# Gate sums of a cross-attention kernel: one accumulator over eight tiles, or two accumulators at output partitions 0 and 64

## What is computed

```python
q = _layernorm(x); k = v = ctx
xc = jnp.concatenate([q, k, v], axis=-1)
ig = (xc @ Wi + bi).transpose(0, 2, 1)[..., None]
fg = (xc @ Wf + bf).transpose(0, 2, 1)[..., None]
log_f = jax.nn.log_sigmoid(fg)
log_f_cum = cumsum(log_f)                        # along the sequence
log_D = causal(log_f_cum[s] - log_f_cum[t]) + ig[t]
D = jnp.exp(log_D - rowmax(log_D))
C = (q_h @ k_h.T / sqrt(32)) * D
h = C / (max(|C.sum|, exp(-rowmax)) + eps) @ v_h  # then normalized per head, scaled
x = x + h
x = x + rms_normalized(down(silu(gate(ln(x))) * up(ln(x))))   # fp4 weights, 512 -> 1408 -> 512
```

## Time and profile before

| | |
|---|---|
| median of 3 runs | 674.09 us (673.83 to 675.59) |
| the profiled execution, its own time | 675.82 us |
| its span in the trace | 674.1 us |
| VectorE busy | 486.1 us, 72% of the span |
| TensorE busy (matmul) | 562.7 us, 83% |
| ScalarE busy | 298.2 us, 44% |
| GpSimd busy | 310.1 us, 46% |
| mean granted TensorE clock | 0.9 of full |

### The profile page before, as it was taken

How to read it: one execution, slowest core, us unless ns; L and a number is a source line. 1 busy time by engine, 2 the same in 40 slices (tenths; PEclk the granted TensorE clock), 3 DMA queues, 4 the chain that set the end, 5 groups by cost and what they waited for, 6 DMA issues and landing times.

```text
span 674.1 us, 7156 instructions
## 1 busy us (share of the span) xinstructions
PE 562.7 (83%) x2254; PEld 298.2 (44%) x2254; DVE 486.1 (72%) x805; ACT 298.2 (44%) x646; POOL 310.1 (46%) x310
## 2 busy tenths in 40 slices
PE   3648698549898897889898896989898897999997
PEld 2326467235464443434554443435464444333443
DVE  4997967987856789756877698836867796189601
ACT  3163446246645531237646612246655611177300
POOL 4222224517635574306746564307646563188600
PEclk9856778959977999899989998889989998999999
DMA  8052011027000110027200110046000000110000
GB/s 218 0 196 87 33 62 64 0 83 263 33 0 1 62 64 0 32 59 271 79 1 0 63 63 0 33 139 237 32 1 0 1 0 1 61 65 0 1 31 32
DMA packets 20880, 39.92 MB, mean 59 GB/s; under 512 B 7274, under 2 KB 7914, under 8 KB 20330
## 3 DMA queue, kind: packets, MB, share of 16 engines
q1 hardware_dynamic: 20842, 39.46, 16.9%
HBM read 30.93 MB, written 4.33 MB: 52 GB/s over the span
## 4 chain that ended last, share of the span: by engine, by line
DVE 41%; PE 27%; issue 15%; POOL 7%; ACT 6%; DMA 2%; SPq 1%; DVEq 0%; POOLq 0%; ACTq 0%
PE pf L887 8%; PE pf L875 6%; DVE ffn L1171 5%; PE pq L788 5%; DVE q_diag L1021 4%; POOL ffn L495 4%; PE po L817 4%; DVE ffn L1175 4%; DVE th L1184 3%; DVE tok L1135 3%; DVE bst L983 2%; ACT ffn L627 2%; ACT dmat L593 2%; DVE hT L1215 2%; DVE dmat L1077 2%
## 5 line engine op out<-in xcount | busy, mean ns | idle before, releaser
L875 PE MATMUL pf<-yT,gu_val 128*128 128x512 f16 x544 | 149.0, 396 | 28.7 <-DVE ffn L1171 17.6
L495 POOL TENSOR_TENSOR ffn<-ffn 128x512 f32<-128x512 f32 x88 | 115.4, 1313 | 118.8 <-ACT ffn L627 118.6
L887 PE MATMUL pf<-w_down,hT 128*128 128x512 f32 x352 | 156.6, 605 | 0.0
L627 ACT ACTIVATE ffn<-pf,gu_scale 128x512 f32<-128x512 f32 x136 | 86.4, 684 | 98.3 <-PE pf L875 72.4
L887 PEld LDWEIGHTS pf<-w_down,hT 128*128 128x128 f32 x352 | 67.9, 194 | 84.5 <-issue 83.4
L875 PEld LDWEIGHTS pf<-yT,gu_val 128*128 128x128 f16 x544 | 47.8, 101 | 108.2 <-DVE ffn L1175 35.0
L593 ACT ACTIVATE dmat<-negm,aT 128x128 f32<-128x128 f32 x256 | 78.1, 396 | 7.0 <-DMA negm<-negm_dram 7.0
L460 POOL TENSOR_SCALAR_AFFINE_SELECT dmat<-dmat 128x512 f32<-128x512 f32 x64 | 45.9, 740 | 69.2 <-ACT dmat L593 69.2
L817 PEld LDWEIGHTS po<-v_sb,dmat 128*128 128x128 f32 x512 | 69.5, 211 | 9.1 <-issue 5.7
L788 PE MATMUL pq<-q_diag,xT 128*128 128x512 f32 x128 | 69.7, 671 | 3.7 <-DVE dmat L1077 2.4
L1077 DVE SCALAR_TENSOR_TENSOR dmat<-pq,dmat 128x512 f32<-128x512 f32 x64 | 43.2, 685 | 35.0 <-PE pq L788 34.5
(11 more groups left out here) (122 smaller groups left out, 751.1 us busy)
## 6 DMA issues: line engine op xcount, KB each, us to landing
negm<-negm_dram SPq DMA_DIRECT2D x32, 512.0 KB, 5.6
ffn<-in_x SPq DMA_DIRECT2D x4, 1024.0 KB, 5.2
ctx_sb<-in_ctx SPq DMA_DIRECT2D x4, 1024.0 KB, 5.2
x_sb<-in_x SPq DMA_DIRECT2D x4, 1024.0 KB, 5.3
x_res<-x_sb SPq DMA_DIRECT2D x4, 1024.0 KB, 4.7
out<-x_res SPq DMA_DIRECT2D x16, 256.0 KB, 2.0
x_res<-in_L_ffn_gate_up_packed SPq DMA_DIRECT2D x1, 704.0 KB, 5.8
th<-in_L_ffn_down_packed SPq DMA_DIRECT2D x1, 352.0 KB, 6.3
```

The source lines that it names most:

```text
L495: pool.tensor_tensor(t, t, ffn[:, 2 * (h % 2) + 1], ALU.add).then_inc(tsum_ready, 1)
L627: act.activation(ffn[:, 2 * (h % 2) + g], bank(q, h, g), ACT.Copy, scale=gu_scale[:, g * GU + o:g * GU + o + 1]).then_inc(t_ready, 1)
L875: last = pe.matmul(bank(q, h, g), gu_val[:, h // 2 + h % 2 * FT, g], yT[:, part, g], start=(part == 0), stop=(part == 1))
L887: last = pe.matmul(pf[:, tt], hT[:, j, tt * P:(tt + 1) * P], w_down[:, j], start=(j == 0), stop=(j == FT - 1))
```

## The change

`gate_sums` issues the same eight products, in another order and to two places: x's tiles accumulate in rows 0 to 47 of the bank, ctx's tiles in rows 64 to 111, one of each in turn. Both kernels' products take up to 64 columns of the array each; the second kernel's use columns 0 to 63 and 64 to 127. `gate_rows` then has to add the two: after each addition of a bias one more `tensor_tensor` adds rows 96 to 111 (forget) or 64 to 79 (input) of the bank. Each of the two is followed by a wait for its own completion.

```diff
 GROWS = DH + NH
+GSIDE = 64
...
-                for k in range(2 * KT):
-                    last = pe.matmul(pm[0:GROWS, :], w_gate[:, k], xT[:, k],
-                                     start=(k == 0), stop=(k == 2 * KT - 1))
+                for k in range(KT):
+                    for side in range(2):
+                        r = side * GSIDE
+                        last = pe.matmul(pm[r:r + GROWS, :], w_gate[:, side * KT + k], xT[:, side * KT + k],
+                                         start=(k == 0), stop=(k == KT - 1))
                 last.then_inc(g_done, 1)
...
                 f = slice(DH, DH + NH)
+                f2 = slice(GSIDE + DH, GSIDE + DH + NH)
                 g2.link(dve.tensor_scalar(gates[:, 1], pm[f, :], bias_col[f], None, ALU.add))
+                g2.link(dve.tensor_tensor(gates[:, 1], pm[f2, :], gates[:, 1], ALU.add))
                 dve.scalar_tensor_tensor(lf[:, 0], gates[:, 1], -1.0, gates[:, 1], ALU.mult, ALU.max
                                          ).then_inc(absf_ready, 1)
                 g2.link(dve.tensor_scalar(gates[:, 0], pm[0:NH, :], bias_col[0:NH], None, ALU.add))
+                g2.link(dve.tensor_tensor(gates[:, 0], pm[GSIDE:GSIDE + NH, :], gates[:, 0], ALU.add))
```

## The result

The changed kernel took 686.04 us (median of 4 runs, 685.19 to 686.68), the kernel before 674.13: ratio 1.017, 95% interval 1.0143 to 1.0198. That is 11.9 us slower; 679.6 was forecast, with 682.8 as the upper end.

The account below looks back on a forecast made before the run. Neither VectorE (41% of the chain) nor TensorE (27%) was the bound by itself, but VectorE was late wherever gates are made. Terms 1.5 + 0.6 + 2.2 + 1.2 = 5.5 us on 674.09 gave 679.6, range 675.6 to 682.8.

Parts of the forecast that it names:

- the idle time before turn_back: TensorE's wait ahead of turn_back was to grow to 6.4 us at pair 2 and 5.7 at pair 3.
- the records behind it: The 12 records of the last down products behind turn_back were to take near 7.1 us at both boundaries.
- TensorE's sums: Gate sums at each pair were to fall from 7.07 to 3.9 us; the saved 3.2 become idle time.
- The step with nine slots of sixteen: In the gate sums, one product's two records cannot overlap each other, so 16 records fill nine slots, 4.0 us.
- The 0.59 us that I took for the upper bound: Duration of one f32 record; if every record of the sums had to finish before the next, 16 give 9.5 us.
- VectorE's additions, 3.6 us of direct delay: Two additions per pair of 0.75 us each were to delay pairs 0 to 3 by 1.5, 0.6, 0.75 and 0.75.
- The working for pair 1: Normalizations starting later lie less beside GpSimd and shorten to 3.0 to 3.1 us, so pair 1 loses 0.6, not 1.5.
- The second addition is hidden: At pairs 2 and 3 VectorE's 1.95 us idle before L1038 hides the second addition, so each pays 0.75 us.
- The sum: 1.5 + 0.6 + 2.2 + 1.2 = 5.5 us; the last two, at pairs 2 and 3, include low clock behind turn_back.
- one more: Rival: one more low clock stretch in a later loop costs up to half of 9.8 us, 683.6; chance 0.06.
- one less: Rival: the 9.8 us low stretch in a loop does not come, winning up to 4.9 us, 674.7; chance 0.13.
- The clock term is absent: Rival: halves not side by side, or clock stays up behind turn_back; only the additions count, 3.6 us, 677.7; chance 0.24.

Follow-up runs that it names:

- The additions alone: Kernel before with VectorE's two bias additions issued twice at every pair, sums unchanged; 684.05 us (ratio 1.0132) and 684.93 us (1.0121).
- Pair 1's doubled additions: Kernel before with VectorE's two bias additions issued a second time at pair 1 only; 678.66 us, +3.5 +-1.7.
- the additions at pairs 2 and 3: Kernel before with VectorE's two bias additions issued a second time at pairs 2 and 3 only; 684.50 us, ratio 1.0117.
- pair 0 alone: Kernel before with VectorE's two bias additions issued a second time at pair 0 only; median 679.03 us against 676.22, by means 0.0 +-2.5.

## Why the prediction was wrong

The direction was right, and so were the idle time before turn_back (6.50 and 6.28 us for 6.4 and 5.7) and the records behind it (7.35 and 7.58 us for 7.1). The size of one term was not.

**TensorE's sums**: right that nobody waits for them, and side by side they ran better than forecast, 3.64 us for 3.9. The step with nine slots of sixteen was wrong, it is eight: the two records of a product each pair with their neighbour of the other half. The 0.59 us that I took for the upper bound is 7.11 / 12 at a partly low clock; in the sums of the kernel before the records start 0.43 us apart.

**VectorE's additions, 3.6 us of direct delay**: right. A grew by 1.41, 0.84, 0.74, 0.73, together 3.7, against 1.5, 0.6, 0.75, 0.75. The working for pair 1 holds a slip: "2.84 + 1.16 x 0.48" adds a number of instructions to a time. Meant is 3.29 us beside GpSimd and 1.16 x 0.48 = 0.56 behind it, 3.85 in all, where 4.02 was seen; that a disturbed normalization takes 1.16 us was an assumption, and the four measured 2.60 for 3.0 to 3.1.

**"The second addition is hidden"** at pairs 2 and 3: right; VectorE idles 1.23 us before L1044 where it was 1.95.

**"The sum", the clock's term of 1.9 us** (2.2 and 1.2, less 0.75 each): this is the term that failed. It was put at 1.9 us and measured 9.3 - 3.7 = 5.6, in two places. First, at the boundaries. B is 7.50, 8.56, 7.59 and 7.45 in the unaltered kernel before, and 9.25, 9.48, 9.65, 10.15, 9.98, 8.92 in the changed one: means 7.8 and 9.6, 1.8 us per boundary, 3.6 in all. At pair 2 it is 2.1 us for a forecast of 1.45, at pair 3 1.5 for 0.45. I took the pair 3 of the one profile, which happened to have its low stretch, as the state of before, and set only 0.45 us of clock cost against it; in eight passages with the gates of pairs 2 and 3 untouched and the sums unshortened (two unaltered profiles and the two with the doubled additions at pair 0 or 1) three had one behind turn_back. The row was right and its use as the normal case was not.

Second, the rest. 9.3 - 3.7 - 3.6 leaves 2.0 us, with the +-1.5 of the 9.3 on it. The profiles put it into the loops only roughly: from L1191 the loops of pairs 2 and 3 are 4.0 us longer together in three profiles of the changed kernel than in two of the kernel before, and one loop alone scatters by 4 to 6 us. I had low stretches there as luck with either sign, 0.06 for one more and 0.13 for one less. For a single profile that is what they are; in the mean they seem not to be. The additions alone cost 8.2 us, with 3.8 direct and about 0.7 more at each boundary (B 8.56 for 7.8): near 3 us are elsewhere, most likely in the loops. Pair 1's doubled additions, 0.7 us of delay, cost 3.5 +-1.7.

That the forecast missed by 6.4 us and not by 3.8 is in part the first four runs of the changed kernel: they came out 11.6 us above the kernel before, the fourteen 9.3. And the 0.3% that I took for what a measurement can tell rested on three runs, which happened to lie within 1.8 us of each other.

**"The clock term is absent" if the halves don't run side by side, 677.7**: wrong as a rival. With the sums at their old length all eight boundary passages with the additions had the low stretch, at 3.07 to 3.12 us of idle at pair 2 and 2.31 to 2.51 at pair 3. In the eight passages without additions there is no sharp point: 1.75, 1.77 and 2.00 us of idle were followed by it, 2.19 to 2.42 (five passages) were not. With the additions it also came behind 2.31, so the length of the idle time alone does not decide it. But with the additions three in eight became eight in eight. I had taken 4.53 us as what suffices, since that was the row I had, and did not price the space between 2.42 and 4.53.

**What stays open**: why a delay seems to shift the mean number of low stretches inside the loops. The gaps there are the same in both kernels (2.1 us, then 1.8 or 2.1), and they are followed by none, 3.4, 6.8 or 10.2 us of low clock. That most of the cost comes with the additions at pairs 2 and 3 is likely from those two alone (+6.4 +-2.7) against pair 0 alone (0.0 +-2.5), and not shown: pair 0's median is 2.8 us up, and pair 1 alone costs 3.5. That the length of a loop goes with the low clock in it is shown by the table of the loops; which alignment decides how much there is, is not.

## What to carry to other kernels

An engine that is early gains nothing from being faster, and TensorE can lose: its shorter sums became idle time, and the clock was low in it and behind it. Before work is taken from TensorE ahead of a wait, count the idle time that results, and move other TensorE work into it (eight products instead of five ahead of turn_back won 2.2 us without the change; eleven regained 5 us with it). More than the idle time holds did not pay here: eleven without the change cost 4.7 us. And where low clock comes behind short gaps in one run and not in the next, one profile shows one outcome: take a second profile of the same kernel before calling any low stretch a state of it, and compare means of ten runs or more, with their intervals.

## What the runs showed of the hardware

Two f32 products of 48 columns into output partitions 0 and 64 run wholly side by side: 16 records in 3.64 us against 7.07, in all four groups. Issued four and four they still took 5.39, with the four pairs of starts listed above. Records of one half never started together in the kernel before (0.43 us apart, all sixteen), so each pair is one record of either half, and records of the second half started ahead of up to three of the first that were issued earlier. The Trainium skill ("TensorE: Matmul & The Clock Gate", Part 3, The mechanism) says that matmuls start and end in strict program order; a strict start would have given 15 steps, 6.6 us, and the measurement speaks against it.

A `tensor_tensor` with one operand in PSUM at partition 96 and the other in SBUF at partition 0 took 0.69 us for 16x512, the same as L1157's 128x512.

VectorE's normalizations, 4.02 us beside GpSimd's four additions, took 2.60 when they started 3.6 us behind GpSimd's first instead of 1.4, and 1.92 alone, while L1036, which now lay beside it, grew from 0.68 to 1.12. The slowdown does not fall on everything: L1038 and L1039, which read PSUM and ran wholly beside GpSimd too, took their usual 0.74 and 0.69. That GpSimd is the cause was not tried by itself.
